# Attention scores of three query blocks as three f32r products of rounded parts and rests

## The reference

```
q, k, v = x @ Wq, x @ Wk, x @ Wv            # 16 heads of 64
q, k = rope(q), rope(k)
sim = q @ k.T * 64**-0.5, causal            # per head, 512 x 512
x1 = layernorm(x + softmax(sim) @ v @ Wo + bo)
w = softmax(x1 @ gate.T + bias); top 2 of 8 experts, normalized
ffn = sum over the chosen experts of w_e * (gelu(x1 @ up_e.T) @ down_e.T)
out = layernorm(x1 + layernorm_no_affine(ffn) + x1)
```

## Time and profile before

| | |
|---|---|
| median of 3 runs | 835.21 us |
| lowest, highest | 835.08, 835.27 us |
| span of the profiled execution | 833.1 us |
| PE busy | 813.1 us (98%) |
| weight loads busy | 587.2 us (70%) |
| DVE busy | 675.5 us (81%) |
| ACT busy | 629.0 us (76%) |
| POOL busy | 553.9 us (66%) |

### The profile page before, as it was taken

One profiled execution on the slowest core, in us unless ns is written; L12 is line 12 of the kernel. 1 busy time (PEld: TensorE's weight loads), 2 busy tenths in 40 slices (PEclk: granted clock), 3 DMA queues, 4 the chain that ended last, 5 costly groups with the idle time before them and its releaser, 6 DMA issues.

```text
span 833.1 us, 21102 instructions
## 1 busy us (share of the span) xinstructions
PE 813.1 (98%) x6267; PEld 587.2 (70%) x6267; DVE 675.5 (81%) x2711; ACT 629.0 (76%) x1672; POOL 553.9 (66%) x612
## 2 busy tenths in 40 slices
PE   8999999999999999999999999999999989999995
PEld 4556667666666666666666666666666669999994
DVE  6787798889888988898889988988898866224996
ACT  4677787888788878887888788878887766555576
POOL 5765646456756775667568866675677336899893
PEclk9999999999999999999999999999999999999998
DMA  5111101000100010001000100010012257424434
GB/s 164 33 40 39 52 20 33 8 20 27 53 14 26 27 40 14 26 28 39 15 27 26 39 15 27 26 39 15 14 36 72 71 143 205 131 82 127 128 114 155
DMA packets 55438, 46.09 MB, mean 55 GB/s; under 512 B 6368, under 2 KB 47072, under 8 KB 55328
## 3 DMA queue, kind: packets, MB, share of 16 engines
q1 hardware_dynamic: 50960, 35.90, 15.0%
q0 software_dynamic: 4224, 8.72, 3.1%
q10 hardware_dynamic: 144, 0.13, 0.1%
HBM read 28.39 MB, written 12.14 MB: 49 GB/s over the span
## 4 chain that ended last, share of the span: by engine, by line
PE 94%; DVE 3%; issue 1%; ACT 1%; DMA 1%; POOL 0%; SPq 0%; DVEq 0%
PE TB L1026 18%; PE S_all L979 18%; PE TB L1010 14%; PE S_all L1177 7%; PE AO L1047 7%; PE TB L1190 4%; PE AO L1190 4%; PE AO L906 4%; PE S_all L1010 3%; PE AO L908 3%; PE AO L907 3%; PE AO L968 1%; PE AO L970 1%; PE AO L969 1%; PE AO L903 1%
## 5 line engine op out<-in xcount | busy, mean ns | idle before, releaser
L1295 ACT ACTIVATE Pr_all<-Sm,nmax 128x512 f32<-128x512 f32 (+3 forms) x512 | 279.6, 550 | 0.0
L1504 DVE CUSTOM_DVE_ANT_0 Sm<-S_all,causal 128x512 f32<-128x512 f32 (+3 forms) x512 | 220.2, 487 | 70.9 <-PE S_all L979 70.8
L665 POOL TENSOR_TENSOR shared<-shared,sin_t 128x512 f32<-128x512 f32 x63 | 80.3, 1275 | 172.3 <-DVE shared L1484 172.1
L1307 ACT ACTIVATE PT<-TB 128x1024 f32<-128x1024 f32 x185 | 130.9, 742 | 63.8 <-PE TB L1010 62.8
L979 PE MATMUL S_all<-kT,qT 64*128 64x512 f32 (+3 forms) x1024 | 166.7, 443 | 1.9 <-POOL kT L668 0.9
L1026 PE MATMUL TB<-PT,shared 128*64 128x128 f32 x1008 | 152.3, 441 | 2.3 <-ACT PT L1307 0.3
L1525 DVE SCALAR_TENSOR_TENSOR x_acc<-AO,rinv,x_acc 128x128 f32<-128x128 f32 x504 | 141.7, 344 | 3.5 <-PE AO L1047 1.2
L1010 PEld LDWEIGHTS TB<-ident,Pr_all 128*128 128x128 f32 x1000 | 108.0, 141 | 38.3 <-ACT Pr_all L1295 21.1
L1010 PE MATMUL TB<-ident,Pr_all 128*128 128x128 f32 x1000 | 133.8, 277 | 0.5 <-ACT PT L1307 0.5
L979 PEld LDWEIGHTS S_all<-kT,qT 64*128 64x128 f32 x1024 | 78.9, 187 | 71.2 <-issue 54.4
L1026 PEld LDWEIGHTS TB<-PT,shared 128*64 128x64 f32 x1008 | 60.5, 136 | 52.0 <-issue 32.7
(11 more groups left out here) (320 smaller groups left out, 1423.9 us busy)
## 6 DMA issues: line engine op xcount, KB each, us to landing
wo<-in_wo SPq DMA_DIRECT2D x64, 64.0 KB, 1.8
PT<-yrows SPq DMA_DIRECT2D x7, 512.0 KB
w_tile<-in_wup SPq DMA_DIRECT2D x10, 256.0 KB
xt<-xrows SPq DMA_DIRECT2D x32, 65.0 KB
x_acc<-in_x SPq DMA_DIRECT2D x8, 256.0 KB
wdown<-in_wdown SPq DMA_DIRECT2D x8, 256.0 KB, 3.2
pay<-pay SPq DMA_DIRECT2D x8, 256.0 KB
x_acc<-pay SPq DMA_DIRECT2D x8, 256.0 KB
```

Source lines behind the costliest of these rows:

```text
L665: nc.gpsimd.tensor_tensor(k_rot, k_rot, sin_t[:, :], ALU.mult).then_inc(k_mul, 1)
L1295: nc.scalar.activation(Pr[j][:, 0:n], Sm[j], ACT.Exp, bias=nmax[:, j:j + 1], scale=-1.0, accum_out=rsum[p][:, h * QB + qb:h * QB + qb + 1] ...
L1307: last = nc.scalar.activation(PT[p][:, :, 0:qb + 1, qb * P:qb * P + P], source, ACT.Copy)
L1504: nc.vector.tensor_tensor_reduce(out=Sm[j], in0=SB[2 * (group % 2) + h][:, at:at + n], in1=causal[:, T - n:T], scale=-0.125, scalar=HUGE, ...
```

## The change

Two constants size packed buffers, and `PLAIN = 2` is the number of first units that keep the old scores.

For the units from 2 on, ACT copies the finished `kT[p]` and the last 384 columns of `qT[p]` into f32r buffers `k_hi[p]` and `q_hi[p]` (the copy rounds). POOL subtracts them from the originals into `k_lo[p]` and `q_lo[p]`, also f32r. The scores of the blocks 1 to 3 are then the sum in PSUM of hi x hi, hi x lo and lo x hi, six matmuls for a block of two heads instead of two. Block 0 (128 keys) stays one f32 product. Inside group 1 block 0 now comes ahead of block 2. PE waits for the splits (`qk_split`) instead of `q_ready` and `k_ready`.

`PT` and `Pr_all` are packed so that they hold only the blocks in use, and `y_all`, `ys_first` and `f_acc` are laid over them and over the new parts.

```diff
+PT_BLOCKS, PR_BLOCKS = 3 * (QB - 1) + QB, QB * (QB + 1) // 2
+PLAIN = 2
...
+        (PT_all, *k_parts), y_all = in_turn(
+            [("PT_all", [P, 2, 2, PT_BLOCKS, P], F32)] + [(f"k_part{i}", [P, T], F32R) for i in range(3)],
+            ("y_all", [P, 2 * 2 * QB * T], F32))
+        (k_part,), ys_first = in_turn([("k_part3", [P, T], F32R)], ("ys_first", [P, 4, C], F32))
+        k_parts.append(k_part)
+        k_hi, k_lo = k_parts[0:2], k_parts[2:4]
...
+        (Pr_all, *q_parts), f_acc = in_turn(
+            [("Pr_all", [P, 2 * PR_BLOCKS * P], F32)] + [(f"q_part{i}", [P, T - P], F32R) for i in range(4)],
+            ("f_acc", [P, NT, C], F32))
+        q_hi, q_lo = q_parts[0:2], q_parts[2:4]
...
+        def pt_written(p, qb):
+
+            return PT_all[:, p, :, qb:4 * qb + 1:3, :]
+
+        def pt_rows(p, h, kb):
+
+            return PT_all[:, p, h, 4 * kb:3 * kb + QB, :].rearrange("k b q -> k (b q)")
...
+            def split_k(u, p):
+
+                pool.wait_ge(qk_high, 2 * (u - PLAIN) + 1)
+                nc.gpsimd.tensor_tensor(k_lo[p][:, :], kT[p][:, :], k_hi[p][:, :], ALU.subtract).then_inc(qk_split, 1)
+
+            def split_q(u, p):
+
+                pool.wait_ge(qk_high, 2 * (u - PLAIN) + 2)
+                nc.gpsimd.tensor_tensor(q_lo[p][:, :], qT[p][:, P:T], q_hi[p][:, :], ALU.subtract).then_inc(qk_split, 1)
...
                     rotate_k(u + 2, p)
                     rotate_q(u + 2, p)
+                    split_k(u + 2, p)
+                    split_q(u + 2, p)
...
-                for i, qb in enumerate(GROUPS[group]):
-                    at = 3 * P * i
+                for qb in sorted(GROUPS[group]):
+                    at, n = 3 * P * GROUPS[group].index(qb), (qb + 1) * P
+                    banks = [SB[2 * (group % 2) + h][:, at:at + n] for h in range(2)]
+                    halves = [slice(D * h, D * h + D) for h in range(2)]
+                    if qb == 0 or u < PLAIN:
+                        for h in range(2):
+                            nc.tensor.matmul(banks[h], qT[p][halves[h], qb * P:qb * P + P], kT[p][halves[h], 0:n],
+                                             start=True, stop=True).then_inc(scored, 1)
+                        continue
+                    rows = slice(qb * P - P, qb * P)
                     for h in range(2):
-                        half = slice(D * h, D * h + D)
-                        nc.tensor.matmul(SB[2 * (group % 2) + h][:, at:at + (qb + 1) * P], qT[p][half, qb * P:qb * P + P],
-                                         kT[p][half, 0:(qb + 1) * P], start=True, stop=True).then_inc(scored, 1)
+                        nc.tensor.matmul(banks[h], q_hi[p][halves[h], rows], k_hi[p][halves[h], 0:n], start=True, stop=False)
+                    for h in range(2):
+                        nc.tensor.matmul(banks[h], q_hi[p][halves[h], rows], k_lo[p][halves[h], 0:n], start=False, stop=False)
+                    for h in range(2):
+                        nc.tensor.matmul(banks[h], q_lo[p][halves[h], rows], k_hi[p][halves[h], 0:n],
+                                         start=False, stop=True).then_inc(scored, 1)
...
-                pe.wait_ge(q_ready, u + 1)
-                pe.wait_ge(k_ready, u + 1)
+                if u < PLAIN:
+                    pe.wait_ge(q_ready, u + 1)
+                    pe.wait_ge(k_ready, u + 1)
+                else:
+                    pe.wait_ge(qk_split, 2 * (u - PLAIN) + 2)
...
+            def high_k(u, p):
+                act.wait_ge(k_ready, u + 1)
+                nc.scalar.activation(k_hi[p][:, :], kT[p][:, :], ACT.Copy).then_inc(qk_high, 1)
+
+            def high_q(u, p):
+                act.wait_ge(q_ready, u + 1)
+                nc.scalar.activation(q_hi[p][:, :], qT[p][:, P:T], ACT.Copy).then_inc(qk_high, 1)
...
+                splits = PLAIN <= u + 1 < UNITS
+                if splits:
+                    high_k(u + 1, 1 - p)
                 if not first:
                     copy_pt(u - 1, 1 - p, 0)
+                if splits:
+                    high_q(u + 1, 1 - p)
                 if 1 <= u <= VBLOCKS - QB:
                     copy_v(QB + u - 1)
...
-                        nc.vector.memset(dst[:, :], eps).then_inc(eps_set, 1)
+                        nc.vector.memset(dst[:, :], eps)
```

More of the change, by code:

```diff
@@ L3 @@
 from contextlib import ExitStack
+from itertools import accumulate
 F32 = mybir.dt.float32
@@ L143, in sb, with in_turn @@
             return ctx.enter_context(nc.sbuf_tensor(name, shape, dtype))
+        def in_turn(first, then):
+            with ExitStack() as attention_only:
+                held = [attention_only.enter_context(nc.sbuf_tensor(*of)) for of in first]
+            return held, sb(*then)
         def ps(name, shape=(P, 512)):
@@ L186, in build_block @@
         q_cos, q_rot, k_cos, k_rot = (shared[:, 2 * QB * VS * P + PAIRS * P + i * T:2 * QB * VS * P + PAIRS * P + i * T + T] for i in range(4))
-        PT = [sb(f"PT{i}", [P, 2, QB, T]) for i in range(2)]
+        (PT_all, *k_parts), y_all = in_turn(
[4 more added lines that the diff above has]
+        k_hi, k_lo = k_parts[0:2], k_parts[2:4]
         OT = [sb(f"OT{i}", [P, T]) for i in range(2)]
@@ L190, in build_block @@
         Sm = [Sm_of[qb][:, h, :] for h, qb in ORDER]
-        Pr_all = sb("Pr_all", [P, BLK, T])
-        Pr = [Pr_all[:, i, :] for i in range(BLK)]
+        (Pr_all, *q_parts), f_acc = in_turn(
+            [("Pr_all", [P, 2 * PR_BLOCKS * P], F32)] + [(f"q_part{i}", [P, T - P], F32R) for i in range(4)],
+            ("f_acc", [P, NT, C], F32))
+        q_hi, q_lo = q_parts[0:2], q_parts[2:4]
+        ends = list(accumulate((qb + 1) * P for h, qb in ORDER))
+        Pr = [Pr_all[:, end - (qb + 1) * P:end] for end, (h, qb) in zip(ends, ORDER)]
         nmax = sb("nmax", [P, BLK])
@@ L1026, in attend @@
                         last = nc.tensor.matmul(o_bank(u)[D * h:D * h + D, kb * P:T], V[u // VS % 2][:, kb, u % VS * P + D * h:u % VS * P + D * h + D],
-                                                PT[p][:, h, kb, kb * P:T], start=(kb == QB - 1), stop=(kb == 0),
+                                                pt_rows(p, h, kb), start=(kb == QB - 1), stop=(kb == 0),
                                                 skip_group_check=True)
@@ L1088, in warm_up @@
                 pe.wait_ge(zeros_set, 1)
-                zeros = PT[0][:, 0, 0, 0:P]
+                zeros = PT_all[:, 0, 0, 0, :]
                 for i in range(WARM):
@@ L1306, in copy_pt @@
                         source = (wide(u) if group else TB)[:, :, 3 * P * i:(3 * i + qb + 1) * P].rearrange("k h (b q) -> k h b q", q=P)
-                    last = nc.scalar.activation(PT[p][:, :, 0:qb + 1, qb * P:qb * P + P], source, ACT.Copy)
+                    last = nc.scalar.activation(pt_written(p, qb), source, ACT.Copy)
                 last.then_inc(pt_ready, 1)
```

12 lines of the change are left out of this document (5 added, 7 removed).

## The result

The changed kernel takes 852.35 us (median of 4 runs, 851.38 to 853.35) where the kernel before takes 835.24 (4 runs, 835.08 to 836.95): a ratio of 1.0203, 95% interval 1.0189 to 1.0217. The forecast was 840.3, with a range up to 850. The direction was right; the loss is 17.1 us instead of 5.1.

The account below looks back on a forecast made before the run. PE was taken to bound attention. From 835.2 us: five normal batches -1.0, first batch -2.3, batch 5 +5.9, batch 7 +2.5, sum +5.1, forecast 840.3 us. Range 828 to 850.

Parts of the forecast that it names:

- What bounds the kernel: Attention units: PE is busy 10.21 of 10.22 us, so PE time saved is time saved unless another engine is late.
- Part 1: Scores on PE, units 2 to 63: f32r pairs side by side at 0.23 us gain 0.36 us a unit.
- Part 2: Two more ACT copies a unit, 0.51 and 0.41 us, mostly fit ACT's idle time; plain units keep about 0.33 us.
- Part 3: ACT's in-order waits for late queries and POOL's overruns give back 25.6 us of the 20.5 us gained on PE.
- Fourth unit: Third-to-fourth unit, batches 1 to 7: queries late behind POOL's normalization stall ACT, then PE, 2.0 us; stretch near 12 us.
- Second unit: Second unit of a batch: late queries and ACT's x rounding leave no gain; 0.1 us lost.
- A normal batch is then +0.2 gained: Batches 1, 2, 3, 4 and 6: 7 x 0.33 - 2.0 - 0.1 each, 1.0 us gained in all five.
- Batch 0 has no such units: First batch: no units with late queries, so 7 x 0.33 = 2.3 us gained.
- Batch 5: Units 40 to 44: POOL overruns by 7.5 us; less 0.6 slack and 1.0 gain, 5.9 us lost.
- 1 (absorbed): Late queries ahead of ACT's value copy partly cost nothing: 833.5 us or faster, 814.7 if all absorbed; chance 0.19.
- 2: Score products of the two heads run one after the other, 0.46 us a pair: 909 us; chance 0.08.
- Rival 3: Weight loads not hidden in a unit's nine score pairs, 1.7 us a unit less 0.36: 919 us; chance 0.04.

Follow-up runs that it names:

- The products alone: The changed kernel with ACT and POOL splitting only units 2 and 3, later scores multiplying those stale parts: 822.71 us, ratio 0.9873.
- POOL's share alone: The changed kernel with POOL subtracting in every unit from 2 on, ACT rounding only units 2 and 3: 837.97 us, ratio 1.0051.

## Why the prediction was right or wrong

**What bounds the kernel: right.** PE's time is the kernel's time where nothing waits, and the changes in single units follow it.

**Part 1: mechanism right, gain mis-sized.** Pairs side by side, loads hidden, block 0 free: all as said. The step that failed is "plain units keep about 0.33 us". They keep 0.17 to 0.20. I priced every product at the 0.23 of a product that follows another f32r product. The first pair of a stretch costs 0.33, and the output projection behind the first scores pays 0.08 more for its first load. The products alone gained 10.7 us, or 11.9 without unit 1 of the first batch, where the forecast has 20.5: 8.6 of the 12 us that the forecast is off.

**Part 2: right.** The copies cost what was said (in the fourth unit the next instruction starts 0.54 and 0.43 us after theirs), and ACT keeps up in plain units.

**Part 3: right in kind, 3.4 us short.** The waits cost 17.1 + 11.9 = 29.0 us, not 25.6.
- Fourth unit: the time is right, 12.34 where I wrote "near 12", but in part by luck. I had PE pay 2.0, all of ACT's stall. It pays 1.4 of a stall of 2.3, and 0.55 for DVE, which the prediction does not have at all. I also left out the keys: ACT's wait for `k_ready` stands ahead of the first copy of probabilities and takes half of the stall.
- Second unit: right in direction, 0.18 lost where I had 0.1.
- "A normal batch is then +0.2 gained": wrong. Batches 1, 2, 3, 4 and 6 lose 0.4 to 2.0 us, 6.7 together. 0.13 too much gain in seven units is 0.9 of it in each batch, the sixth unit 0.5 in four of them (the DVE operation), and the third unit of batches 3 and 6 0.9 and 0.5 (10.91 and 10.58 beside 10.05). In the turn before these POOL has table arithmetic (277.74 to 280.11 in batch 3) that I looked for only in batches 5 and 7.
- First batch: forecast 2.3 gained, measured 0.2. Six units gain 0.19 to 0.25, and unit 1 loses 1.16. "Batch 0 has no such units" was the failing step: there ACT waits 1.1 for the queries of unit 2, and PE 1.05 for the value copy behind it (PE's timeline of the changed kernel):

```profile
26.87 1.10 PE L940 MATMUL AO<-x1T,w_tile 128*128 128x512 f32 x2 [1.05 <-ACT shared L1335]
```

- Batch 5: 8.15 lost, forecast 5.9. POOL's overrun was sized about right, 7.5 forecast and 8.5 measured up to turn 44. The failing step is what I took off, 0.6 of slack and 1.0 of gain: PE follows POOL's queue to its unit 45, so the overrun arrives nearly whole, and only units 46 and 47 gain their 0.2. That the granted clock stays at 1.00 ("so I leave it there") was wrong as well, but it costs the batch nothing that the runs show. Batch 7: 3.20, forecast 2.5.

**Rivals.** 1 (absorbed): for the most part no; in the fourth unit PE pays 1.4 of ACT's stall of 2.3. 2 and 3: no, the pairs at 0.24 rule out both. Rival 3 rests on the page "TensorE: Matmul & The Clock Gate" of the Trainium skill; with the heads in either order, the trace does not agree with its rule here. The end of the range, 850, left out that both errors, in gain and in waits, go the same way. It also had a slip in it: 0.2 us more of ACT in 50 units is 10 us, not 5.

## What to carry to other kernels

Price a cheaper instruction from rows in which its neighbours are the ones that it will have: the first of a run, and the instruction behind the run, can cost more than the run's own step, and 0.1 us a unit was half the gain here. When an engine gets more work, list each in-order queue behind every new wait, also the queue that waits back; the units where that queue is already full pay for all the others, and leaving the change out of those units (and moving one subtraction) turned 2% slower into 0.8% faster. When work moves on one engine, look at what its neighbours on the same memory do at that moment. And before a slow clock is charged with a loss, look whether the next wait would have taken the time anyway.

## What the runs showed of the hardware

- f32r products of 64 rows, two heads, 512 columns: 0.24 us for a pair, 0.33 for the first; the order of the heads in the program makes no difference (1.0213 and 1.0203), both start together.
- A small DVE operation with both operands in SBUF ends with the POOL subtraction that it meets: 1.71 us instead of 0.19 (396.13), 0.75 instead of 0.16 (372.48, 128x4). POOL's subtractions, where they are done, add some 20 us of DVE busy time: 696.2 (change) and 701.2 (POOL's share alone), against 677.5 and 675.1 in the two kernels that do them only in units 2 and 3.
- The granted clock fell to 0.50 within a gap of 3.64 us in PE and stayed there for 5.2 us, although PE was busy again all that time. After a gap of 3.65 us in the kernel that subtracts x sooner it was still 1.00 for 1.1 us of work and then 0.50 for 3.41. In the kernel with POOL's share alone it was 0.50 in the stretch behind the gap of 2.01 us as well (468.20 to 474.20); behind a gap of 1.62 us in batch 7 of the changed kernel it stayed at 1.00.
